# Queries loaded step by step, a sixth place for keys, a fourth for turned input, and spare products of the whole array in chunk 0 of an attention block

## The chip, the cores and the metric

The kernel runs on one core of one Trainium2 chip. A core has a matrix engine (TensorE, PE in the profile; its weight loads are PEld), VectorE (DVE), ScalarE (ACT), GpSimd (POOL), and SyncE (SP), which here issues every transfer. What is compared is device time in microseconds; lower is better.

## What is computed

One transformer layer on x of shape (2, 2048, 256): normalise, causal attention with 16 heads of 16 and 4 key heads, and beside it a linear map through the Fourier domain; both are added to x.

```python
xn = _layernorm(x)                          # x: (2, 2048, 256)
q = (xn @ wq).reshape(B, S, 16, 16); k = (xn @ wk).reshape(B, S, 4, 16); v = (xn @ wv).reshape(B, S, 4, 16)
q, k = _apply_rope(q, cos, sin), _apply_rope(k, cos, sin)
k, v = broadcast to 16 heads
scores = jnp.einsum('bshd,bthd->bhst', q, k) * scale    # causal mask, -inf above
out = jnp.einsum('bhst,bthd->bshd', softmax(scores), v).reshape(B, S, 256) @ wo
y = real(ifft(fft(xn) @ (w_re + i w_im))) + bias
x = x + out + y
```

## The kernel before

**Tiles.** The 4096 rows are cut into 8 chunks of 512 (`CHUNKS`), 4 for each of the two batches (`NJ`). In a chunk there are 4 steps, one for each key head, so 32 steps n, with n // 4 the chunk. Step n works on 4 heads, two in the upper half of the array's rows and two in the lower. Chunk 0 and chunk 4 see only themselves, chunk 3 and chunk 7 see four chunks of keys. A step has 4 x (j + 1) units (j the chunk's place in its batch), one for each tile of 128 keys.

**The work of a step.** First come the maxima ("a"): TensorE multiplies queries by keys into one of two pairs of banks in `psA`, and VectorE takes the maximum over each row (`reduce`, lines 1083 and 1085). Each such use has two halves (o = 1, 0). After the last one `shift` makes a value per row that SP carries back into the queries as two more rows (`load_shift`, 8 small transfers), so that the scores come out shifted. Then the scores ("b", line 1319) go into one of the three banks of `psS`, ScalarE takes their exponential (`exps`, line 956), GpSimd masks the diagonal, and the values product ("pv", line 1333) adds into `psO` over the units of a step: four matmuls side by side, each on 32 columns of the array (`VW`). `copy_sums` takes the finished sums to `oraw`, which has places for 8 steps.

**Around it.** For each chunk the input is normalised on GpSimd (`n`), turned ("t"), projected to keys and queries ("qk", line 1246, three of them) and values ("v"), and rotated on GpSimd in six steps (`rotate`). The rotated parts are stored to memory (`store`) and loaded again in another layout: `load_k` into one of `KS` = 5 places of `k_st`, `load_q` all four steps of a chunk at once into one of two halves of `q_st`. Both wait in SP's queue for the steps that use the old content (`pv_done`); a key load from chunk 5 on waits for all of batch 0. Behind the attention come "e", "e2", "e3": turn the sums, divide, project, and add to x.

**What sets the order.** `schedule()` simulates the engines with made-up durations and writes the order of TensorE, GpSimd and SP once and for all; ScalarE's and VectorE's follow from it. On the chip each engine runs its list in order, and a waiting instruction holds back all behind it. The opening (tables for the rotation, the Fourier weights, projections of chunk 0) is written by hand and stands ahead. VectorE reads the second batch's input for its moments right behind step 1's `shift` (`STATS_AT` = 1, lines 1034 and 1037), from `oraw`, which is still free.

## Time and profile before

| | us |
|---|---|
| median of 3 runs | 1062.55 (1062.13 to 1066.18) |
| the profiled execution | 1059.53 |
| its span, first to last instruction | 1057.5 |

A row of the profile's page gives an engine's busy time and its share of the span. A table of stretches gives, for windows counted from the span's start, how much each engine was busy in it and the clock that TensorE was granted, as a share of full speed. A row of the list in order of time gives start, duration, engine, line and tiles, how often, and in brackets how long the engine had been idle and who released it. A matmul of 32-bit numbers shows as two matmuls.

### The profile page before, as it was taken

The numbers are of one execution on the slowest core, as the hardware profiler recorded it, in microseconds if no ns is written. First come the engines' busy times: TensorE is split into PE (matmuls) and PEld (weight loads), VectorE is DVE, ScalarE is ACT, GpSimd is POOL, SyncE is SP. The second block draws the span as 40 slices with busy tenths as digits, with TensorE's granted clock in tenths as the row PEclk, the third lists the DMA queues.
The fourth block names the chain that finished last, engine by engine and source line by source line (L and its number), as shares of the span: only waits on it lengthen the run. The fifth ranks groups of instructions, "written<-read, shape, count | busy, mean of one in ns | idle before, by whom it ended". The sixth has DMA issues, their size and how long they took to land.

```text
span 1057.5 us, 17589 instructions
## 1 busy us (share of the span) xinstructions
PE 995.1 (94%) x6792; PEld 492.2 (47%) x6792; DVE 739.3 (70%) x893; ACT 651.8 (62%) x1303; POOL 321.7 (30%) x348
## 2 busy tenths in 40 slices
PE   8879799999999989999999899998999998999988
PEld 7635455444544434534444445444454443444434
DVE  6685867677678886778870367666768888778801
ACT  3324456646567745667777456663667774677785
POOL 6485851147380000183001258135010000110000
PEclk9866969999999979999999899988899997999999
DMA  5756070003610042100004314400700000000000
GB/s 159 139 145 74 31 111 11 13 20 83 99 36 17 1 59 32 42 22 30 2 4 54 47 42 87 65 3 30 111 22 1 2 1 1 12 11 2 1 1 20
DMA packets 35666, 43.46 MB, mean 41 GB/s; under 512 B 9344, under 2 KB 21248, under 8 KB 35584
## 3 DMA queue, kind: packets, MB, share of 16 engines
q1 hardware_dynamic: 35584, 42.35, 21.2%
q8 instruction: 53, 0.87, 0.3%
q14 instruction: 29, 0.24, 0.1%
HBM read 27.13 MB, written 14.68 MB: 40 GB/s over the span
## 4 chain that ended last, share of the span: by engine, by line
PE 80%; ACT 7%; DVE 7%; issue 3%; DMA 1%; POOL 1%; SPq 0%; ACTq 0%; POOLq 0%
PE psO L1333 27%; PE psA L1272 18%; PE psS L1319 17%; ACT prob_sb L956 5%; PE psS L1246 4%; DVE pmax L1085 3%; PE psS L1304 3%; PE psS L1306 2%; DVE pmax L1083 2%; PE psA L1277 2%; DMA q_st<-parts_scratch 1%; PE psS L1253 1%; PE psA L1287 1%; PE psO L1376 1%; ACT oraw_sb L965 1%
## 5 line engine op out<-in xcount | busy, mean ns | idle before, releaser
L956 ACT ACTIVATE prob_sb<-psS 128x512 f32<-128x512 f32 (+2 forms) x1108 | 561.7, 588 | 268.0 <-PE psS L1319 264.9
L1085 DVE TENSOR_REDUCE pmax<-psA 128x2 f32<-128x1024 f32 x384 | 458.6, 1220 | 117.7 <-PE psA L1272 116.6
L1319 PE MATMUL psS<-q_st,k_st 50*128 50x512 f32 (+3 forms) x1232 | 406.7, 440 | 8.4 <-ACT prob_sb L956 7.2
L1272 PE MATMUL psA<-k_st,q_st 48*128 48x512 f32 (+3 forms) x1280 | 371.4, 443 | 32.0 <-DVE pmax L1085 15.0
L1333 PE MATMUL psO<-prob_sb,v_sb 128*32 128x512 f32 (+3 forms) x2560 | 315.0, 566 | 12.5 <-ACT prob_sb L956 8.2
L1272 PEld LDWEIGHTS psA<-k_st,q_st 48*128 48x128 f32 x1280 | 180.7, 200 | 265.3 <-DVE pmax L1085 107.5
L1083 DVE TENSOR_REDUCE pmax<-psA 128x4 f32<-128x512 f32 (+2 forms) x192 | 198.9, 1043 | 97.1 <-PE psA L1277 95.6
L842 POOL TENSOR_SCALAR_AFFINE_SELECT prob_sb<-prob_sb 128x512 f32<-128x512 f32 x128 | 81.1, 636 | 562.9 <-ACT prob_sb L956 562.6
L1319 PEld LDWEIGHTS psS<-q_st,k_st 50*128 50x128 f32 x1232 | 200.2, 196 | 111.6 <-ACT prob_sb L956 101.1
L1333 PEld LDWEIGHTS psO<-prob_sb,v_sb 128*32 128x32 f32 x2560 | 51.6, 110 | 100.4 <-issue 43.1
L1277 PE MATMUL psA<-mask_r,mask_l 64*128 64x64 bf16 (+1 forms) x768 | 83.0, 217 | 0.0
L1246 PE MATMUL psS<-xnT,w_sb 128*128 128x512 f32 x96 | 50.9, 659 | 0.8 <-ACT xnT L911 0.8
L833 POOL TENSOR_TENSOR x_sb<-x_sb,back_sb 128x256 f32<-128x256 f32 x28 | 20.5, 731 | 84.7 <-ACT back_sb L941 84.7
L1277 PEld LDWEIGHTS psA<-mask_r,mask_l 64*128 64x128 bf16 x768 | 40.1, 103 | 11.9 <-issue 2.7
L919 ACT ACTIVATE qc<-psS 128x512 f32<-128x512 f32 x24 | 14.4, 599 | 49.4 <-PE psS L1246 46.6
L809 POOL TENSOR_TENSOR turn<-qc,cos_sb 128x512 f32<-128x512 f32 x21 | 26.7, 1272 | 48.8 <-ACT qc L919 47.4
L941 ACT ACTIVATE back_sb<-psS 128x256 f32<-128x256 f32 x28 | 10.8, 384 | 39.5 <-PE psS L1306 39.5
L1304 PE MATMUL psS<-m_sb,xnT 128*128 128x256 f32 x112 | 32.6, 415 | 0.0
L1113 DVE RECIPROCAL rl<-psA 128x32 f32<-128x32 f32 x14 | 5.0, 354 | 39.0 <-PE psA L1287 39.0
L789 POOL TENSOR_SCALAR xn<-x_sb,stat,rstd 128x256 f32<-128x256 f32 x24 | 29.0, 1224 | 4.9 <-PE psS L1238 3.9
L1189 DVE RECIPROCAL rl<-psS 128x16 f32<-128x16 f32 x4 | 1.0, 250 | 42.0 <-PE psS L1356 42.0
L1306 PE MATMUL psS<-wo_sb,back_sb 128*128 128x256 f32 x112 | 29.4, 386 | 0.0
(104 smaller groups left out, 582.9 us busy)
## 6 DMA issues: line engine op xcount, KB each, us to landing
q_st<-parts_scratch SPq DMA_DIRECT2D x42, 256.0 KB, 12.0
parts_scratch<-parts SPq DMA_DIRECT2D x64, 128.0 KB
k_st<-parts_scratch SPq DMA_DIRECT2D x48, 128.0 KB, 4.6
q_st<-spartT SPq DMA_DIRECT2D x256, 2.0 KB
x_sb<-in_L_attn_x SPq DMA_DIRECT2D x7, 512.0 KB, 4.2
out<-x_sb SPq DMA_DIRECT2D x14, 256.0 KB, 2.2
parts_scratch<-parts SPq DMA_DIRECT2D x32, 64.0 KB
oraw_sb<-in_L_attn_x SPq DMA_DIRECT2D x1, 2048.0 KB, 14.7
```

The costliest lines, as they stand in the source:

```text
L789: nc.gpsimd.tensor_scalar(xn[:, i, :], x_sb[:, xt(cc, i), :], stat[:, t, 0:1], rstd[:, t:t + 1], ALU.subtract, ALU.mult).then_inc(S["xn_re ...
L842: nc.gpsimd.affine_select(out=blk, in_=blk, compare_op=ALU.is_ge, fill=0.0, base=0, pattern=[[0, R], [1, P]], channel_multiplier=-1).then_ ...
L956: nc.scalar.activation(prob[:, g % DEEP, r0:r0 + hp, s0:CH], bank_at(bank)[:, 0:hp * w].rearrange("p (h s) -> p h s", h=hp), ACT.Exp).then ...
L1083: nc.vector.reduce_max(to, psA[:, two:two + 2, 0:per * w].rearrange("p o (h s) -> p o h s", h=per), AX.X).then_inc(S["a_free"], 1)
L1085: nc.vector.reduce_max(pmax[:, heads[0]:heads[0] + 3:2, i, q], psA[:, two:two + 2, :], AX.X).then_inc(S["a_free"], 1)
L1246: last = mm(bank, w_sb[:, c, block_cols(m)], xnT[:, cc % 3, c, :], start=(c == 0), stop=(c == KC - 1))
L1272: last = mm(bank[:, k * w:(k + 1) * w], q_st[lo:lo + ROWS, n % (2 * KV), heads[o * per + k] % 2, i * P:(i + 1) * P], k_st[lo:lo + ROWS, sl ...
L1277: last = mm(to, mask_l[lo:lo + HALF, h, :], mask_r[lo:lo + HALF, h:h + 1, :].broadcast_to([HALF, per, HALF]), start=False, stop=h == 1)
L1304: mm(bank[:, 0:D], xnT[:, cc % 3, c, t * P:(t + 1) * P], m_sb[:, c, :], start=(c == 0), stop=False)
L1306: last = mm(bank[:, 0:D], o_nT[:, i, c * P:(c + 1) * P], wo_sb[:, c, :], start=False, stop=(c == KC - 1))
L1319: last = mm(bank[:, h * w:(h + 1) * w], k_st[lo:lo + FULL, key_slot(n, tile), kv, tile % CT * P:(tile % CT + 1) * P], q_st[lo:lo + FULL, n ...
L1333: last = mm(psO[32 * r:32 * r + VW, s0:CH], v_sb[:, key_slot(n, tile) * CT + tile % CT, n % KV, :], prob[:, g % DEEP, r, s0:CH], start=(u ...
```

## The change

- `KS` goes from 5 to 6 places for keys, `xnT` from 3 to 4 for turned input (`XS`). The room comes from `oraw` (6 steps in place of 8, `OS`), `turn` (one row of 512 in place of two; the other product goes into `parts`), and from the value matrix, whose rows are 17 wide (`VW`) instead of 32. `psO` still holds four groups 32 apart (`GW`); VectorE clears it once at the start.
- Queries are loaded by step: 6 transfers of 64 KB for step n, waiting for step n - 8, each place with its own semaphore.
- Since a rotation's second product goes into `parts`, GpSimd waits for the store of two rotations earlier at the rotation's second step instead of its fifth. `copy_sums` waits for the turning of the sums of six steps earlier instead of eight. The second batch's input is read in two transfers, the second into the fourth place of `xnT`.
- `spare(at)` multiplies a 128x128 block of weights by 512 columns of input into the bank that the next real product will overwrite; nobody reads the result. Four stand ahead of the first maxima, and the planner puts one ("w") wherever, in its own reckoning, the next job of steps 0 to 3 is more than 0.6 us away and a bank is free. There are twelve of these: seven between the maxima from step 0's last to step 2's second, and five later up to step 2's scores.
- The planner takes all this into account, so the order changes everywhere.

The core of the diff:

```diff
-    KS = NJ + 1
+    KS = NJ + 2
+    XS = 4
+    OS = 6
+    TWO = OS * CH // D
...
+    SPARE_TO, SPARE_FROM, SPARE_TOOK = KV, 0.6, 0.87
+    OPEN_SPARES = 4
     LAG = 2
     DEEP = 3
-    VW = 32
+    VW = HD + 1
+    GW = 32
...
+                over = (chunk_begin(NJ) if cc >= KS else 0) if job[0] == "kload" else BEGIN[max(job[1] - 2 * KV + 1, 0)]
+                if len(pv_at) < over:
+                    continue
+                gate = max(gate, pv_at[over - 1] if over else 0.0)
                 if gate <= now:
-                    loads.remove(cc)
-                    issue_dma(gate, ("kload", cc))
-                    issue_dma(gate, ("qload", cc))
+                    loads.remove(job)
+                    issue_dma(gate, job)
...
-            return max(slot_ready(), q_ready.get(A_USES[next_a][1] // KV, big))
+            return max(slot_ready(), q_ready.get(A_USES[next_a][1], big))
...
+            if step < SPARE_TO and ready[choice if choice != "x" else "b"] > now + SPARE_FROM and bank_ready() <= now and a_part == 1:
+                pe.append(("w", len(ring)))
+                full("full", SPARE_TOOK, now)
+                continue
...
-        oraw_sb = sb("oraw_sb", [P, 2 * KV * CH], fp32)
-        oraw = oraw_sb[:, :].rearrange("p (n s) -> p n s", s=CH)
-        x_two = oraw_sb[:, :].rearrange("p (t n) -> p t n", n=D)
+        oraw = sb("oraw_sb", [P, OS, CH], fp32)
...
-        xnT = sb("xnT", [P, 3, KC, CH], fp32)
+        xnT = sb("xnT", [P, XS, KC, CH], fp32)
+        x_last = xnT[:, XS - 1, :, :].rearrange("p c s -> p (c s)").rearrange("p (t n) -> p t n", n=D)
...
-        turn = sb("turn", [P, 2, CH], fp32)
+        turn = sb("turn", [P, CH], fp32)
...
+            def load_q(n, t):
+                cc, g = n // KV, n % KV
                 m = 3 * cc + 1 + t
                 sp.wait_ge(stored[m % 2], 16 * (stores_before(m) + 4))
-                if cc >= 2:
-                    sp.wait_ge(S["pv_done"], chunk_begin(cc - 1))
+                if n >= 2 * KV:
+                    sp.wait_ge(S["pv_done"], BEGIN[n - 2 * KV + 1])
+                at = slice(t * P + 2 * g * HD, t * P + 2 * (g + 1) * HD)
                 for row, part in enumerate(PART_ROWS):
-                    slot = cc % 2 * KV
-                    sp.dma_start(q_st[t * HALF + row * HD:t * HALF + (row + 1) * HD, slot:slot + KV, :, :].rearrange("d g r s -> d (g r) s").bitcast(fp32),
-                                 scratch[cc, part, t * P:(t + 1) * P, :].rearrange("(h d) s -> d h s", d=HD)).then_inc(q_in[cc % 2], 16)
+                    sp.dma_start(q_st[t * HALF + row * HD:t * HALF + (row + 1) * HD, n % (2 * KV), :, :].bitcast(fp32),
+                                 scratch[cc, part, at, :].rearrange("(h d) s -> d h s", d=HD)).then_inc(q_in[n % (2 * KV)], 16)
...
-            sp.dma_start(x_two, x_v[:, BTILES:2 * BTILES, :]).then_inc(S["x_two_in"], 16)
+            sp.dma_start(x_two, x_v[:, BTILES:BTILES + TWO, :]).then_inc(S["x_two_in"], 16)
+            sp.dma_start(x_last, x_v[:, BTILES + TWO:2 * BTILES, :]).then_inc(S["x_two_in"], 16)
...
                 elif s == 1:
                     pool.wait_ge(S["turn_done"], base + 1)
-                    nc.gpsimd.tensor_tensor(turn[0:HALF, 1, :], qc[HALF:P, m % 2, :], sin_sb[HALF:P, span], ALU.mult).then_inc(S["turn_done"], 1)
+                    pool.wait_ge(stored[m % 2], 16 * stores_before(m))
+                    nc.gpsimd.tensor_tensor(other[0:HALF, :], qc[HALF:P, m % 2, :], sin_sb[HALF:P, span], ALU.mult).then_inc(S["turn_done"], 1)
...
+                if cc == XS - 1 and c == 0:
+                    act.wait_ge(S["bn_ready"], CHUNKS * CT)
+                if cc >= XS and c == 0:
+                    act.wait_ge(S["bank_full"], BANK["e3", cc - XS, 1, 1] + 1)
+                nc.scalar.activation(xnT[:, cc % XS, c, :], psS[:, BANK["t", cc, c] % RING, :], ACT.Copy).then_inc(S["bank_free"], 1)
...
-                if n >= 2 * KV:
-                    act.wait_ge(S["a_full"], back_job(2 * (n // KV - 2) + 1) + 1)
+                if n >= OS:
+                    act.wait_ge(S["a_full"], back_job(2 * ((n - OS) // KV) + 1) + 1)
...
+            nc.vector.memset(psO[:, :], 0.0).then_inc(S["psO_zeroed"], 1)
...
-                if m == 0 and n == 0 and o == 1:
-                    pe.wait_ge(S["q_first_in"], 96)
-                    pe.wait_ge(k_in[0], 96)
-                elif m == 0 and g == (1 if cc == 0 else 0) and o == 1:
-                    pe.wait_ge(q_in[cc % 2], 96 * (cc // 2 + 1))
-                    pe.wait_ge(k_in[cc % 2], 96 * (cc // 2 + 1))
+                if m == 0 and o == 1:
+                    if n in (0, 1):
+                        pe.wait_ge(q_in[n], 96)
+                    elif n >= KV:
+                        pe.wait_ge(q_in[n % (2 * KV)], 96 * q_loads(n))
+                    if g == 0:
+                        pe.wait_ge(k_in[cc], 96)
...
-                    last = mm(psO[32 * r:32 * r + VW, s0:CH], v_sb[:, key_slot(n, tile) * CT + tile % CT, n % KV, :], prob[:, g % DEEP, r, s0:CH],
-                              start=(u == 0), stop=(u == len(UNITS[n]) - 1), tile_position=(0, 32 * r))
+                    last = mm(psO[GW * r:GW * r + VW, s0:CH], v_sb[:, key_slot(n, tile) * CT + tile % CT, n % KV, :], prob[:, g % DEEP, r, s0:CH],
+                              start=(u == 0), stop=(u == len(UNITS[n]) - 1), tile_position=(0, GW * r))
...
+            def spare(at):
+                last = turn_before(at, LATE)
+                if last >= 0:
+                    pe.wait_ge(S["bank_free"], last + 1)
+                mm(bank_at(at), w_sb[:, 0, block_cols(0)], xnT[:, 0, 0, :], start=True, stop=True)
...
-                mm(psO[:, 0:P], ident[:, :], ident[:, :], start=True, stop=True)
+                mm(psA[:, 3, 0:P], ident[:, :], ident[:, :], start=True, stop=True)
...
+            for _ in range(OPEN_SPARES):
+                spare(len(OPENING))
...
+                elif job[0] == "w":
+                    spare(job[1])
```

What moves, at three places. TensorE, from the last maxima of step 0 to the first two of step 1. The rows `psA<-k_st,q_st` are maxima, `psA<-mask_r,mask_l` their mask. Before:

```order
L1272 MATMUL psA<-k_st,q_st 128x512 [waits a_free]
L1277 MATMUL psA<-mask_r,mask_l 128x64 x2
L1272 MATMUL psA<-k_st,q_st 128x128 [waits a_free,k_in_0,q_in_0]
L1272 MATMUL psA<-k_st,q_st 128x128
L1277 MATMUL psA<-mask_r,mask_l 128x2x64 x2
L1272 MATMUL psA<-k_st,q_st 128x128 [waits a_free]
```

Now, with line 1380 a spare product:

```order
L1300 MATMUL psA<-k_st,q_st 128x512 [waits a_free]
L1305 MATMUL psA<-mask_r,mask_l 128x64 x2
L1380 MATMUL psS<-xnT,w_sb 128x512 [waits bank_free]
L1300 MATMUL psA<-k_st,q_st 128x128 [waits a_free,q_in1]
L1300 MATMUL psA<-k_st,q_st 128x128
L1305 MATMUL psA<-mask_r,mask_l 128x2x64 x2
L1300 MATMUL psA<-k_st,q_st 128x128 [waits a_free]
L1300 MATMUL psA<-k_st,q_st 128x128
L1305 MATMUL psA<-mask_r,mask_l 128x2x64 x2
L1380 MATMUL psS<-xnT,w_sb 128x512 [waits bank_free]
```

A whole-array product now stands ahead of seven of the eight uses from step 1's first to step 2's second.

TensorE, step 0's scores (`psS<-q_st,k_st`) and first values (`psO<-prob_sb,v_sb`). Before:

```order
L1319 MATMUL psS<-q_st,k_st 128x384 [waits bank_free] x4
L1319 MATMUL psS<-q_st,k_st 128x256 [waits bank_free]
L1319 MATMUL psS<-q_st,k_st 128x256
...
L1272 MATMUL psA<-k_st,q_st 128x384 [waits a_free]
L1277 MATMUL psA<-mask_r,mask_l 128x64 x2
L1272 MATMUL psA<-k_st,q_st 128x384 [waits a_free]
L1277 MATMUL psA<-mask_r,mask_l 128x64 x2
L1333 MATMUL psO<-prob_sb,v_sb 32x512 [waits diag_masked]
L1333 MATMUL psO<-prob_sb,v_sb 32x512 x3
```

Now:

```order
L1347 MATMUL psS<-q_st,k_st 128x384 [waits bank_free] x4
L1364 MATMUL psO<-prob_sb,v_sb 17x512 [waits diag_masked,psO_zeroed]
L1364 MATMUL psO<-prob_sb,v_sb 17x512 x3
L1347 MATMUL psS<-q_st,k_st 128x256 [waits bank_free]
L1347 MATMUL psS<-q_st,k_st 128x256
...
L1364 MATMUL psO<-prob_sb,v_sb 17x384 [waits diag_masked]
L1364 MATMUL psO<-prob_sb,v_sb 17x384 x3
L1300 MATMUL psA<-k_st,q_st 128x384 [waits a_free]
L1305 MATMUL psA<-mask_r,mask_l 128x64 x2
```

Before, the first values product stood behind maxima that need a buffer back from VectorE (`a_free`), which by then reads the moments; now the first two value products stand ahead of the next maxima.

SP, around the last steps of chunk 3 (`q_st<-spartT` is `shift`, `k_st<-parts_scratch` a load of keys, `q_st<-parts_scratch` one of queries). Before, after the shifts of steps 15 to 19:

```order
L696 DMA q_st<-spartT 2x8x32 [waits spartT_ready]
L696 DMA q_st<-spartT 2x8x32 x7
L667 DMA k_st<-parts_scratch 16x4x512 [waits pv_done,ones_ready,stored_1]
L667 DMA k_st<-parts_scratch 16x4x512 x5
L677 DMA q_st<-parts_scratch 16x8x512 [waits pv_done,stored_0]
L677 DMA q_st<-parts_scratch 16x8x512 x2
L677 DMA q_st<-parts_scratch 16x8x512 [waits pv_done,stored_1]
L677 DMA q_st<-parts_scratch 16x8x512 x2
```

Now the same keys are loaded between queries of steps 18 and 19, ahead of step 12's shift:

```order
L698 DMA q_st<-parts_scratch 16x2x512 [waits pv_done,stored_1]
L698 DMA q_st<-parts_scratch 16x2x512 x2
L698 DMA q_st<-parts_scratch 16x2x512 [waits pv_done,stored_0]
L698 DMA q_st<-parts_scratch 16x2x512 x2
L687 DMA k_st<-parts_scratch 16x4x512 [waits ones_ready,stored_1]
L687 DMA k_st<-parts_scratch 16x4x512 x5
L717 DMA q_st<-spartT 2x8x32 [waits spartT_ready]
L717 DMA q_st<-spartT 2x8x32 x7
L698 DMA q_st<-parts_scratch 16x2x512 [waits pv_done,stored_1]
L698 DMA q_st<-parts_scratch 16x2x512 x2
L698 DMA q_st<-parts_scratch 16x2x512 [waits pv_done,stored_0]
L698 DMA q_st<-parts_scratch 16x2x512 x2
```

The key load no longer waits for `pv_done`; the queries are loaded for one step at a time. Counted in the order, 373 uses of maxima stood ahead of step 23's first scores and 389 do now (398 and 402 at step 24, 494 and 493 at step 28).

## Rows read from the trace of the kernel before

**Rows 1.** The page's first part for TensorE, and the list of cores.

```profile
PE 995.1 (94%) x6792; PEld 492.2 (47%) x6792; DVE 739.3 (70%) x893; ACT 651.8 (62%) x1303; POOL 321.7 (30%) x348
core 0: 1057.5 us, clock 0.932
```

**Rows 2.** Groups by line and shape: count, busy us, mean ns, idle before.

```profile
L1085 DVE TENSOR_REDUCE pmax<-psA 128x2 f32<-128x1024 f32 x384 | 458.6, 1220 | 117.7 <-PE psA L1272 116.6
L1272 PE MATMUL psA<-k_st,q_st 48*128 48x512 f32 x896 | 287.3, 476 | 16.4 <-DVE pmax L1085 11.7 <-DMA q_st<-parts_scratch 2.7 <-DVE pmax L1083 1.4
L1333 PE MATMUL psO<-prob_sb,v_sb 128*32 128x512 f32 x1792 | 249.9, 631 | 12.5 <-ACT prob_sb L956 8.2 <-ACT oraw_sb L965 2.6
```

**Rows 3.** Stretches: length, PE, PEld, DVE, ACT, POOL busy, clock, DMA.

```profile
61.00:96.00 35.00, 30.64 (x176) 17.22 (x176) 24.39 (x55) 12.96 (x27) 24.62 (x24) 0.50 0.65 101
71.00:74.40 3.40, 0.00 (x0) 0.00 (x0) 3.33 (x23) 0.62 (x2) 3.27 (x4) 0.50 0.14 34
101.60:124.80 23.20, 21.26 (x191) 11.44 (x190) 18.78 (x21) 16.03 (x32) 18.57 (x20) 1.00 0.07 21
124.80:129.30 4.50, 1.94 (x26) 1.02 (x18) 4.37 (x7) 0.00 (x0) 4.12 (x4) 0.94 0.22 75
129.30:152.30 23.00, 21.60 (x102) 10.93 (x102) 17.29 (x19) 10.77 (x21) 16.33 (x11) 0.50 0.84 122
```

**Rows 4.** TensorE in order of time, opening, and scores of steps 2 and 4.

```profile
38.68 1.88 PE L1246 MATMUL psS<-xnT,w_sb 128*128 128x512 f32 x4
...
44.40 0.70 PE L1272 MATMUL psA<-k_st,q_st 48*128 48x128 f32 x4 [3.84 <-issue]
...
46.05 3.78 PE L1246 MATMUL psS<-xnT,w_sb 128*128 128x512 f32 x4
...
101.73 0.73 PE L1319 MATMUL psS<-q_st,k_st 50*128 50x512 f32 x2
...
133.52 0.63 PE L1319 MATMUL psS<-q_st,k_st 50*128 50x512 f32 x2
```

**Rows 5.** SP in order of time: loads of chunk 1, shifts.

```profile
75.25 2.90 SPq L667 DMA_DIRECT2D k_st<-parts_scratch  x6
78.20 2.79 SPq L677 DMA_DIRECT2D q_st<-parts_scratch  x6
...
87.86 2.65 SPq L696 DMA_DIRECT2D q_st<-spartT  x4
...
126.58 5.22 SPq L696 DMA_DIRECT2D q_st<-spartT  x8
```

**Rows 6.** Transfers: count, KB each, median us from issue to landing.

```profile
q_st<-parts_scratch SPq DMA_DIRECT2D x42, 256.0 KB, 12.0
...
q_st<-parts_scratch SPq DMA_DIRECT2D x6, 64.0 KB, 2.5
```

**Rows 7.** SP and TensorE in order of time, between chunks 3 and 5.

```profile
570.60 2.68 SPq L667 DMA_DIRECT2D k_st<-parts_scratch  x6
...
591.19 0.50 PE L1272 MATMUL psA<-k_st,q_st 48*128 48x512 f32 x2 [2.69 <-DMA q_st<-parts_scratch]
```

**Rows 8.** Stretches later in the program, columns as in rows 3.

```profile
552.00:588.00 36.00, 32.79 (x214) 15.50 (x211) 1.11 (x3) 25.19 (x53) 5.89 (x9) 1.00 0.50 62
...
592.00:603.50 11.50, 11.50 (x65) 6.78 (x60) 5.60 (x5) 5.00 (x10) 1.91 (x3) 0.55 0.00 0
732.00:746.00 14.00, 9.68 (x52) 5.02 (x44) 12.85 (x15) 2.57 (x6) 4.22 (x4) 0.65 0.24 72
736.60:750.00 13.40, 11.88 (x54) 6.39 (x54) 10.47 (x10) 4.60 (x9) 0.00 (x0) 0.50 0.54 105
870.00:886.00 16.00, 12.13 (x68) 5.73 (x66) 14.25 (x17) 5.12 (x10) 0.00 (x0) 0.70 0.01 2
...
701.30:705.70 4.40, 3.92 (x24) 2.38 (x23) 3.66 (x4) 4.33 (x9) 3.35 (x4) 0.99 0.00 0
705.70:715.80 10.10, 10.10 (x46) 3.81 (x45) 4.37 (x4) 3.92 (x9) 4.86 (x5) 0.50 0.06 21
```

96 lines of the change are left out of this document (50 added, 46 removed).

## The prediction

> **What bounds the kernel now.** Read the page first, then the list of cores. TensorE has something to do in 94% of the span, and its mean granted clock is 0.932 [rows 1]. Since it has only the levels 1.2 and 2.4 GHz, about 2 x 0.068 x 1057.5 = 144 us pass at the lower one. So TensorE is the bound, and there are two things to win: its holes, and the time in which it does the same work at half speed. The next engine is VectorE, whose reduction over 1024 columns takes 1220 ns against some 0.5 us for the TensorE pair that feeds it [rows 2]: wherever TensorE has only such pairs left, it waits.
>
> The table of stretches shows where this happens first [rows 3]. From 61 to 96 us the clock is 0.50; TensorE shows 30.64 of 35 us busy, which would be about 15.3 at full clock, and VectorE needs 24.39. In the middle lies a hole of 3.40 us (71.0 to 74.4) in which VectorE reads the second half of the input. From 124.8 to 129.3 TensorE works 1.94 of 4.5 us, since VectorE is late, and then 23.00 us pass at 0.50 again, with 21.60 busy. The single instructions show the opening [rows 4]: TensorE waits 3.84 us for the first queries, and the projection behind it takes 3.78 us instead of 1.88. The scores of step 2 begin at 101.73, those of step 4 at 133.52.
>
> Later there are three more places. From 552 to 588 us VectorE has 1.11 us of work in 36 [rows 8]: chunk 5's maxima need its keys and queries, and those are fetched only once chunk 3 is through (570.60); TensorE waits 2.69 us for them [rows 7], and 592.0 to 603.5 runs at 0.55 [rows 8]. At the entries to chunks 6 and 7 VectorE is busy 12.85 of 14.00 and 14.25 of 16.00 us and TensorE only 9.68 and 12.13, with the clock at half behind the first [rows 8].
>
> **The opening.** Four spare products stand ahead of the first maxima. One is half of the row with four instructions, 1.88 / 2 = 0.94 us; four are 3.8 us in a hole of 3.84 [rows 4]. They cost 0 to 0.3 us. If they hold the clock, the 3.78 us become 1.9, and VectorE was waiting for this work: 1.9 us won.
>
> Behind it come seven spares between the maxima of steps 0 to 2. A pair takes about 0.7 us with its masks, a spare 0.94, together 1.6, against 0.7 to 1.2 us of VectorE: now and then TensorE is late. I count 0.9 us lost for the seven (bounds 0, where VectorE's buffer of two covers them, and 7 x 0.5 = 3.5). The net is 1.0 us by the end of step 1.
>
> **The rest of chunk 0.** In the new order the first value products no longer stand behind a product that waits for VectorE's moments, so 3.40 us of idle time [rows 3] are used. The clock is the larger part. Kept up, it would turn 30.64 us into 15.3, but VectorE's 24.39 us then bound the 35.00, so at most 10 us can be won; and five more spares (4.7 us) and eight pairs of step 4 (4 us) stand ahead of step 2's scores. These pairs are not extra, they leave later, the spares don't. Between the last spare of step 1 and the first values lie only scores and maxima, the same mix with which the clock was lost at 705.7 us, while TensorE was busy for 3.92 of 4.40 us [rows 8]. So I expect it to fall there too, for part of the stretch. I put step 2's scores at 101 to 107 us (101.73 before), but with eight pairs of maxima done ahead. From there to step 4's scores is some 22 us of work (23.20 before, [rows 3]), without the wait for VectorE: 123 to 129 us instead of 133.52. I take 127: **6.5 us won** (bounds 4 and 10).
>
> With step 4's maxima ready early the hole at 124.8 goes, and so may the 23.00 us at 0.50. At full clock the 21.60 us busy would be 10.8, but VectorE has 17.29 in them [rows 3]; at best 5.7 us are won, and I take **5** (bounds 0 and 5.7).
>
> **Queries step by step.** A load of 256 KB lands after 12.0 us, one of 64 KB in just the new shape after 2.5 [rows 6]. So a step's queries arrive some 10 us sooner. The price is issue time on SP: six issues take 2.79 us [rows 5], and a chunk now has 24, or 11.2 us: 8.4 more, and the maxima that SP carries into the queries (`shift`) are queued behind. In chunk 1 loads would end at 75.25 + 2.9 + 11.2 = 89.4 instead of 81; step 2's maxima, sent from 87.86 before, then go out from about 89.4. Step 4's went out at 126.58 and its scores began 6.9 us later [rows 4, 5], so step 2's scores are free at 96 to 97, still before TensorE comes to the scores (101 or later). Cost 0; if TensorE came there at 95 it would be 2. At chunk 2's entry SP has one query load, one store of four issues and one `shift` behind the last values of step 7, about 2.8 + 2 + 6.9 = 12 us; the TensorE order has about 18 us of other work there (five projections, four turnings and eleven pairs). Cost 0.
>
> The Trainium skill speaks against such a split: DMA: Bandwidth & Descriptors (Bandwidth) advises batching transfers to 1 MiB or more and calls small ones descriptor-dominated. The trace has both sizes, and 4 x 2.5 us is not more than 12.0 [rows 6]; by the rule the loads would land later and the next gain would be none.
>
> **One more place for keys.** With six places, chunk 5's keys don't wait for chunk 3 any more, and its first queries wait only for step 12. VectorE can then work in the 36 us in which it now has 1.11. What TensorE does is not less, so the gain is its idle 2.69 us and the 11.50 us at 0.55, of which 10 are at half clock and 5 are lost: 7.7, and I take **7.5** (bounds 2.7 and 9) [rows 7, 8].
>
> **Entries to chunks 6, 7 and 2.** By the new order 389 maxima are issued when step 23's scores begin, where there were 373, and step 24 needs 390. So the wait at 732 to 746 (14.00 - 9.68 = 4.3 us) should go, and with it the half clock (11.88 busy of 13.40, some 5 us) [rows 8]. I take **4**, for VectorE's 12.85 us were needed somewhere (bounds 0 and 9). Before step 28 the counts are 494 and 493 and only the way there is smoother: **1** (0 to 8). Chunk 2's inputs come earlier: 0.5 to 1, I take **1**.
>
> **Costed at nothing.** The value matrix is 17 wide instead of 32: its products stream the same 512 columns, 631 ns each [rows 2]. The clearing of psO and the second DMA of the input lie in VectorE's and SP's waits. GpSimd's wait for a store moves from the fifth step of a rotation to the second; behind it masks and additions are queued, for which the values wait, but the store is two rotations old. ScalarE's copy of the sums waits for the turning of the sums of six steps earlier, with exponentials behind it; in the TensorE order that turning stands ahead. If either wait bites, it is once in a chunk, some 1 us each: 0 to 8 us in all, and I take 0.
>
> The sum is 6.5 + 5 + 7.5 + 4 + 1 + 1 = 25 us. The profiled execution took 1059.53 us (span 1057.5), so it would take 1034.5; the median of the runs shown is 3.0 above it, and by the median the time is 1062.55 - 25 = 1037.5, or **1038 us**.
>
> **Rivals.** First, *the first chunk gives little*: the clock falls at step 0's scores and stays down to the first projection; the spares then cost 1.9 us apiece and take back what their holes gave. The gain is that of the later places and a little more, 14 us: 1048. For it speaks that TensorE was busy for 10.10 us on end at 0.50 without rising [rows 8].
>
> Second, *the holes only move*: VectorE and TensorE together have as much to do as before, and what is not waited for at one entry is waited for at the next: 1060. Against it speaks that VectorE is idle for 36 us on end.
>
> Third, on the other side, *the narrower values cost clock*. The clock was lost in a stretch that held only maxima and scores (50 rows of the array), and TensorE was busy in it [rows 8]. If the 128 x 32 value products are what holds it elsewhere, and if it is the columns at work in them that matter, 17 of 32 may not do. Each us at half clock costs up to half a us (3.78 against 1.88, [rows 4]), so from 2 x 25 = 50 us more at half clock the gain is gone; with 150 us more the time is 1038 + 75 = 1113. Nothing in this trace tells columns from array tiles.
>
> The Trainium skill gives another reading in TensorE: Matmul & The Clock Gate (Part 1): activity releases the throttle, whatever its kind. The trace does not agree, as TensorE was at 0.50 with 10.10 of 10.10 us busy; by that rule the third rival would be void and spares of any kind would do.
>
> **How the numbers follow.** Forecast (1025 to 1044) 0.42; more than that, where the entries to chunks 6 and 7 both clear, 0.12; little from the first chunk (1044 to 1056) 0.25; holes only move 0.08; narrower values or another new wait make it slower 0.13. For the range I leave out the slow case and the lowest few per cent: 1020 to 1062. The measurement of this kernel can tell about 0.5% (5.3 us) from no change: faster 0.79, same 0.08, slower 0.13.
>
> **What would show it.** Right: clock 1.0 at 46 to 50 us; step 2's scores at 101 to 107 and step 4's at 123 to 129; VectorE busy between chunk 3's end and chunk 5's start, no wait there for a query load; no wait for VectorE at chunk 6's entry. Wrong: a mean clock below 0.93, value products of 1.9 us in the later chunks (third rival); step 4's scores at 132 or later (first); `shift` loads late on SP behind query loads, with scores waiting for them.

## Result, and the profile after

| | median | runs | profiled span | mean clock |
|---|---|---|---|---|
| before | 1063.04 us | 1062.13 to 1066.18 | 1057.5 | 0.932 |
| after | 1022.62 us | 1017.43 to 1023.73 | 1020.8 | 0.958 |

The change makes the kernel faster by 3.9%: ratio 0.9614, 95% interval 0.9575 to 0.9652. The forecast was 1038 us, and the range of 1020 to 1062 holds the time. The sign was right; the gain was 40 us, not 25, and came from other places than forecast. Here and below a median is of all runs of a kernel, while a ratio leaves out those over 1.5% above its fastest, since the runs of one kernel can differ by 3% (1044.61 to 1074.18 us in e5).

The page after, for TensorE, with the granted clock in 40 slices, and the list of cores (to be set beside [rows 1]):

```profile
PE 982.8 (96%) x6824; PEld 475.0 (47%) x6824; DVE 732.6 (72%) x894; ACT 650.3 (64%) x1303; POOL 325.4 (32%) x350
...
PEclk9987789999989997999899999999999999999999
...
core 0: 1020.8 us, clock 0.958
```

TensorE is idle for 1020.8 - 982.8 = 38.0 us (62.4 before) and at half clock for 2 x 0.042 x 1020.8 = 86 us (144 before). Most of what is still lost stands in the first half: the last 20 slices all read 9.

Where the 36.7 us of span went shows in a table of stretches. Their bounds are the ends of steps, read from ScalarE's copy of the sums of steps 4, 11, 15, 23 and 27. The end of a step means this copy from here on. Columns: stretch, length, busy time of PE, PEld, DVE, ACT, POOL, clock, DMA share, GB/s. Before:

```profile
0.00:161.90 161.90, 141.11 (x886) 86.46 (x887) 114.47 (x222) 67.98 (x127) 100.30 (x102) 0.79 0.54 108
161.90:387.90 226.00, 215.93 (x1515) 103.66 (x1513) 175.84 (x184) 143.14 (x290) 79.59 (x82) 0.98 0.17 35
387.90:571.40 183.50, 178.11 (x1252) 80.51 (x1251) 127.21 (x141) 130.02 (x258) 41.07 (x43) 0.96 0.14 25
571.40:743.90 172.50, 160.62 (x1098) 83.45 (x1097) 104.73 (x118) 92.23 (x192) 74.58 (x81) 0.91 0.30 52
743.90:883.40 139.50, 133.04 (x932) 63.08 (x930) 113.67 (x119) 92.73 (x187) 13.09 (x20) 0.95 0.16 24
```

After, for the same steps:

```profile
0.00:161.50 161.50, 153.71 (x944) 90.37 (x945) 111.06 (x223) 70.13 (x133) 105.94 (x110) 0.87 0.42 101
161.50:396.40 234.90, 224.32 (x1524) 103.53 (x1523) 173.79 (x184) 143.69 (x290) 97.84 (x95) 0.96 0.23 55
396.40:579.60 183.20, 180.26 (x1318) 82.62 (x1317) 144.04 (x161) 129.65 (x258) 41.20 (x43) 0.96 0.07 22
579.60:717.40 137.80, 133.13 (x1018) 68.29 (x1017) 92.69 (x104) 89.69 (x189) 48.40 (x58) 0.99 0.14 35
717.40:847.10 129.70, 125.60 (x908) 56.77 (x906) 106.04 (x112) 91.60 (x185) 18.87 (x26) 0.99 0.14 32
```

- **Chunk 0 and step 4: 0.4 us.** TensorE is busier (153.71 of 161.5 against 141.11 of 161.9) and its clock better, 0.87 against 0.79, and yet the stretch is as long. A second profile of the changed kernel (e9 below) has 159.2 us here.
- **Steps 5 to 11: 8.9 us lost**, TensorE busy for 8.4 us more at a clock of 0.96 against 0.98.
- **Steps 12 to 15: 0.3 us.** But VectorE has 144.04 us of work here and not 127.21: maxima of chunk 5, done ahead.
- **Steps 16 to 23: 34.7 us.** Most of the gain is here. Of it 7 us are TensorE's idle time (11.9 against 4.7) and some 14 the half clock (2 x 0.09 x 172.5 = 31 us against 2 x 0.01 x 137.8 = 3, each us of them worth half a us, an estimate); the other 13 or 14 us are work that now stands earlier (1018 matmuls here against 1098, and 1318 against 1252 in steps 12 to 15).
- **Steps 24 to 27: 9.8 us**; steps 28 to 31: 0.4.

The first chunk in the order of time, TensorE after (compare [rows 4]); spares are L1380 (two matmuls each, so the four of the opening show as x8), maxima L1300, values L1364, scores L1347, projections L1273 and, for the values, L1280:

```profile
40.83 3.60 PE L1380 MATMUL psS<-xnT,w_sb 128*128 128x512 f32 x8
...
45.57 1.98 PE L1273 MATMUL psS<-xnT,w_sb 128*128 128x512 f32 x4
...
68.98 1.91 PE L1364 MATMUL psO<-prob_sb,v_sb 128*17 128x512 f32 x8 [1.38 <-POOL prob_sb L866]
...
115.98 2.39 PE L1280 MATMUL psS<-w_sb,xnT 128*128 128x64 f32 x10 [1.56 <-ACT prob_sb L982]
...
133.44 0.49 PE L1347 MATMUL psS<-q_st,k_st 50*128 50x512 f32 x1
```

And the stretches that answer to [rows 3] and [rows 8]; the second is the new one at half clock:

```profile
61.00:96.00 35.00, 32.79 (x204) 16.19 (x204) 24.27 (x60) 12.53 (x27) 25.33 (x23) 0.71 0.44 101
116.50:133.40 16.90, 16.58 (x98) 10.17 (x97) 9.39 (x14) 6.45 (x14) 9.43 (x10) 0.51 0.10 33
552.00:588.00 36.00, 35.51 (x308) 18.27 (x300) 28.55 (x36) 25.69 (x54) 3.83 (x7) 1.00 0.10 23
732.00:746.00 14.00, 13.77 (x110) 6.58 (x102) 10.38 (x11) 9.93 (x20) 1.41 (x3) 1.00 0.67 118
```

The opening went as forecast: four spares in 3.60 us, the projection at 45.57 in 1.98 us and not 3.78. But the clock falls just ahead of the first values (it is 0.73 from 68.0 to 68.5 us and 0.50 behind that), inside a hole of 1.38 us in which TensorE waits for GpSimd's mask. It falls again at 116.0 (0.52 from 116.0 to 116.5), at the end of a hole of 1.56 us in which TensorE waits for ScalarE to free a bank for the values' projection. In e9, the same kernel, the first fall comes just before 66 us, with TensorE busy for 0.94 of the 1.00 us ahead, and the second again at the end of the wait for ScalarE (1.58 us, until 113.69). Step 4's scores begin at 133.44 (133.52 before).

Later, two things have changed. SP after, at the keys of chunks 5, 6 and 7, and the keys of chunks 6 and 7 before (chunk 5's were issued at 570.60, [rows 7]):

```profile
360.07 2.72 SPq L687 DMA_DIRECT2D k_st<-parts_scratch  x6
...
585.31 2.70 SPq L687 DMA_DIRECT2D k_st<-parts_scratch  x6
...
735.96 2.88 SPq L687 DMA_DIRECT2D k_st<-parts_scratch  x6
```

```profile
651.68 2.71 SPq L667 DMA_DIRECT2D k_st<-parts_scratch  x6
...
743.34 2.82 SPq L667 DMA_DIRECT2D k_st<-parts_scratch  x6
```

Chunk 5's keys are fetched 210 us sooner, chunk 6's 66. And so VectorE isn't idle any more between 552 and 588 us. Its two long waits before, and its longest of that stretch after (start, length, what it does, idle time ahead and what ended it):

```profile
574.27 0.36 DVE L1113 RECIPROCAL rl<-psA 128x32 f32<-128x32 f32 x1 [23.22 <-PE psA L1287]
...
588.11 0.36 DVE L1113 RECIPROCAL rl<-psA 128x32 f32<-128x32 f32 x1 [12.69 <-PE psA L1287]
```

```profile
581.64 1.23 DVE L1111 TENSOR_REDUCE pmax<-psA 128x2 f32<-128x1024 f32 x1 [2.72 <-PE psA L1300]
```

A useful measure of this is VectorE's **lead**: how long before the end of step n - 1 the maxima of step n are complete (its `smax` row). For step 20 these rows are, before and after (step 19 ends at 629.14 and at 623.44):

```profile
618.05 0.18 DVE L1092 TENSOR_REDUCE smax<-pmax 128x16 f32<-128x32 f32 x1
```

```profile
576.36 0.19 DVE L1118 TENSOR_REDUCE smax<-pmax 128x16 f32<-128x32 f32 x1
```

At steps 20, 24 and 28, where chunks 5, 6 and 7 begin, the lead was 11.1, 9.6 and 9.4 us before; it is 47.1, 22.9 and 8.3 after. At step 8 it has become worse, from 2.1 to -5.3: there the last maxima now come after the end of step 7.

### The profile page after: what moved, and what is told of

Its sections match the earlier page's. It is cut to its first block, busy times and chain, and to the rows that moved or that the text cites. A ratio compares the mean times of both kernels' runs of the same rounds, so it can differ in the third digit from the quotient of the medians.

```text
span 1020.8 us, 17825 instructions
## 1 busy us (share of the span) xinstructions
PE 982.8 (96%) x6824; PEld 475.0 (47%) x6824; DVE 732.6 (72%) x894; ACT 650.3 (64%) x1303; POOL 325.4 (32%) x350
## 4 chain that ended last, share of the span: by engine, by line
PE 82%; ACT 7%; DVE 3%; issue 2%; POOL 1%; DMA 1%; SPq 1%; POOLq 0%; ACTq 0%; DVEq 0%
PE psO L1364 28%; PE psA L1300 19%; PE psS L1347 17%; ACT prob_sb L982 5%; PE psS L1273 3%; PE psS L1332 3%; PE psS L1334 2%; DVE pmax L1111 2%; PE psA L1305 2%; PE psA L1315 1%; PE psS L1280 1%; DVE pmax L1109 1%; ACT oraw_sb L991 1%; PE psA L1347 1%; PE psS L1265 1%
## 5 line engine op out<-in xcount | busy, mean ns | idle before, releaser
L1111 DVE TENSOR_REDUCE pmax<-psA 128x2 f32<-128x1024 f32 x384 | 459.6, 1220 | 134.1 <-PE psA L1300 132.7
L1347 PE MATMUL psS<-q_st,k_st 50*128 50x512 f32 (+3 forms) x1232 | 403.5, 431 | 5.0 <-ACT prob_sb L982 3.5
L1300 PE MATMUL psA<-k_st,q_st 48*128 48x512 f32 (+3 forms) x1280 | 362.3, 427 | 7.8 <-DVE pmax L1111 5.0
L1364 PE MATMUL psO<-prob_sb,v_sb 128*17 128x512 f32 (+3 forms) x2560 | 310.4, 558 | 15.2 <-ACT prob_sb L982 7.5
L1300 PEld LDWEIGHTS psA<-k_st,q_st 48*128 48x128 f32 x1280 | 177.6, 192 | 252.4 <-DVE pmax L1111 96.4
L1347 PEld LDWEIGHTS psS<-q_st,k_st 50*128 50x128 f32 x1232 | 196.8, 192 | 96.3 <-ACT prob_sb L982 84.0
L1364 PEld LDWEIGHTS psO<-prob_sb,v_sb 128*17 128x17 f32 x2560 | 43.2, 96 | 106.1 <-issue 44.8
L1305 PE MATMUL psA<-mask_r,mask_l 64*128 64x64 bf16 (+1 forms) x768 | 79.2, 210 | 0.0
L1273 PE MATMUL psS<-xnT,w_sb 128*128 128x512 f32 x96 | 46.8, 614 | 0.8 <-ACT xnT L937 0.8
L837 POOL TENSOR_TENSOR parts<-qc,sin_sb 64x512 f32<-64x512 f32 x21 | 26.7, 1271 | 6.1 <-DMA parts_scratch<-parts 3.7
## 6 DMA issues: line engine op xcount, KB each, us to landing
oraw_sb<-in_L_attn_x SPq DMA_DIRECT2D x1, 1536.0 KB, 11.9
```

The costliest lines, as they stand in the source:

```text
L1111: nc.vector.reduce_max(pmax[:, heads[0]:heads[0] + 3:2, i, q], psA[:, two:two + 2, :], AX.X).then_inc(S["a_free"], 1)
L1273: last = mm(bank, w_sb[:, c, block_cols(m)], xnT[:, cc % XS, c, :], start=(c == 0), stop=(c == KC - 1))
L1300: last = mm(bank[:, k * w:(k + 1) * w], q_st[lo:lo + ROWS, n % (2 * KV), heads[o * per + k] % 2, i * P:(i + 1) * P], k_st[lo:lo + ROWS, sl ...
L1305: last = mm(to, mask_l[lo:lo + HALF, h, :], mask_r[lo:lo + HALF, h:h + 1, :].broadcast_to([HALF, per, HALF]), start=False, stop=h == 1)
L1347: last = mm(bank[:, h * w:(h + 1) * w], k_st[lo:lo + FULL, key_slot(n, tile), kv, tile % CT * P:(tile % CT + 1) * P], q_st[lo:lo + FULL, n ...
L1364: last = mm(psO[GW * r:GW * r + VW, s0:CH], v_sb[:, key_slot(n, tile) * CT + tile % CT, n % KV, :], prob[:, g % DEEP, r, s0:CH], start=(u ...
```

## Experiments

All ratios are to the kernel before, timed beside them on the same chip; 1% is 10.6 us. The table below has them in one place. The planner lays out a new order for each kernel that is told of another limit, so "a part undone" is that part with the order that goes with it; only the runs in which the text says so keep the order. What an order alone can be worth is 7 us, plus or minus 7 (e10 and e11).

| label | key places | input places | queries released | spares | median us | ratio (95%) |
|---|---|---|---|---|---|---|
| changed kernel, first time | 6 | 4 | by step | 4 + 12 | 1022.62 | 0.9614 (0.9575 to 0.9652) |
| e9, changed kernel again | 6 | 4 | by step | 4 + 12 | 1018.39 | 0.9597 (0.9563 to 0.9631) |
| e1 | 6 | 4 | by step | none | 1010.85 | 0.9552 (0.9474 to 0.9631) |
| e2 | **5** | 4 | by step | 4 + 12 | 1030.70 | 0.9746 (0.9674 to 0.9818) |
| e3 | 6 | **3** | by step | 4 + 12 | 1067.25 | 1.0074 (1.0033 to 1.0114) |
| e4 | 6 | 4 | **by chunk** | 4 + 12 | 1045.89 | 0.9859 (0.9795 to 0.9923) |
| e5 | 5 | 3 | by chunk | none | 1051.22 | 0.9886 (0.9852 to 0.9919) |
| e6 | 5 | **4** | by chunk | none | 1035.29 | 0.9769 (0.9720 to 0.9818) |
| e7 | 5 | 3 | **by step** | none | 1066.71 | 1.0053 (1.0028 to 1.0079) |
| e8, values 32 wide | 5 | 4 | by step | 4 + 12 | 1049.33 | none given |
| e10 | 6 | 4 | by step | none | 1012.27 | 0.9563 (0.9526 to 0.9601) |
| e11, order of the changed kernel | 6 | 4 | by step | **left out** | 1024.09 | 0.9630 (0.9579 to 0.9682) |
| e12 | 6 | 4 | by step | 4 + 0 | 1008.52 | 0.9553 (0.9508 to 0.9598) |

### One part undone: spares, key place, input place, release of the queries

**e1.**

```diff
-    SPARE_TO, SPARE_FROM, SPARE_TOOK = KV, 0.6, 0.87
-    OPEN_SPARES = 4
+    SPARE_TO, SPARE_FROM, SPARE_TOOK = 0, 0.6, 0.87
+    OPEN_SPARES = 0
```

> The changed kernel without its spare matmuls, neither the four in the opening nor those that the planner puts in holes of the first chunk; the other parts stay. The comparison of the two traces has the start of the copy of step 4's sums at 161.94 us before and 161.48 after, so the first chunk gave nothing by there. Theory A (the spares are worth about nothing, since the clock falls between them all the same): 1020 to 1026 us, with the first projection of chunk 1's third block back near 3.8 us (it took 3.78 before and 1.98 after). Rival B (the spares hold the clock through steps 0 and 1, and the shorter opening, 82.11 against 89.69 us at the end of step 0, is theirs, and what the planner did with it later too): 1027 to 1035 us.

Measured: 1010.85 us, which neither theory had: without spares the kernel was not as fast but, by the ratios, some 0.6% faster, with intervals that overlap. The first projection of chunk 1's third block took 2.94 us, on the way to the 3.8 expected. This is taken up again in e9 to e12.

**e2.**

```diff
-    KS = NJ + 2
+    KS = NJ + 1
```

> The changed kernel with five places for keys and values in place of six; queries, input places, width and spares as changed. The planner is told that the keys of chunk 5 wait for the end of step 15, and lays out its order by that. Theory A (the sixth key place frees the entry to the second batch, which is where the time went: from the end of step 15 to the end of step 19 the kernel before took 57.7 us and the changed one 43.8): 14 us of the gain go, 1033 to 1040 us, with the wait of TensorE near 591 us on the keys' transfer back, at a half clock behind it. Rival B (the fourth input place does the work, by letting the stages run further ahead): within 5 us of the changed kernel, 1018 to 1028 us.

Measured: 1030.70 us, ratio 0.9746 against 0.9597 to 0.9614 for the changed kernel: the sixth key place is worth 14 to 16 us in this company. Chunk 5's keys are issued at 558.65, at the end of step 15, and VectorE waits for them again:

```profile
558.65 2.65 SPq L687 DMA_DIRECT2D k_st<-parts_scratch  x6
```

```profile
562.32 0.36 DVE L1139 RECIPROCAL rl<-psA 128x32 f32<-128x32 f32 x1 [21.34 <-PE psA L1315]
```

Theory A's size was right (14 us expected; its 1033 to 1040 us was missed by 2 on the low side), its place only half: the wait of TensorE for a transfer is 1.0 us and not 2.69, and the lead at step 24 falls from 22.9 to 11.3 us too.

**e3.** The fourth place stays in memory, for the last tiles of the statistics' input.

```diff
+    XM = 3
-   ... xnT[:, cc % XS, ...]
+   ... xnT[:, cc % XM, ...]
-                if cc >= XS:
-                    at = max(at, e3_at.get((cc - XS, 1, 1), big))
+                if cc >= XM:
+                    at = max(at, e3_at.get((cc - XM, 1, 1), big))
```

> The changed kernel with the normed input's places used in turns of three, as before; the fourth holds only the last tiles of the second batch for the statistics. Six key places, queries by the step, narrow values and spares stay. Theory A (the fourth place carries the entries to chunks 5, 6 and 7: steps 20 to 27 took 107.4 + 7.4 us more in the kernel before, of 254.3 against 223.7): about 25 to 30 us of the gain go, 1045 to 1053 us, with the half clock back at the entries to chunks 6 and 7. Rival B (key place and queries by the step do it, and the fourth place only shifts work between stages that are full anyway): 1018 to 1030 us.

Measured: 1067.25 us. All of the gain is gone, and more: 49 us, where theory A had 25 to 30. (Steps 20 to 27 took 254.3 us before and 223.7 after, 30.6 less; the "107.4 + 7.4" of the expectation is a slip.) The rows name the mechanism: chunk 6's keys are issued at 706.52 (585.31 after the change, 651.68 before it), VectorE has nothing to do for 63.63 us, and when the work comes TensorE, ahead with everything else, waits for it at half clock.

```profile
706.52 2.80 SPq L686 DMA_DIRECT2D k_st<-parts_scratch  x6
```

```profile
718.12 1.23 DVE L1108 TENSOR_REDUCE pmax<-psA 128x2 f32<-128x1024 f32 x1 [63.63 <-PE psA L1297]
```

```profile
740.00:750.00 10.00, 6.33 (x26) 2.70 (x26) 10.00 (x10) 0.00 (x0) 0.01 (x1) 0.66 0.96 149
750.00:760.00 10.00, 6.76 (x30) 3.10 (x28) 9.56 (x13) 0.00 (x0) 0.00 (x0) 0.50 0.76 115
```

The lead at step 24 is -32.8 us. Chunk 5's maxima were early (lead 50.9 at step 20): with key place and queries released, VectorE ran ahead into chunk 5 and then stood still for chunk 6. This is the "holes only move" of the forecast's second rival, with its price.

**e4.** The loads keep their size and their number; only what they wait for is as before.

```diff
-                    sp.wait_ge(S["pv_done"], BEGIN[n - 2 * KV + 1])
+                    sp.wait_ge(S["pv_done"], chunk_begin(cc - 1))
```

> The changed kernel whose loads of queries still go one step at a time (four pairs of transfers a chunk), but all four of a chunk wait for the same thing as before the change, the end of the chunk two before it, and the planner is told so. Theory A (release by the step matters where the queries' places come free late, at each entry to a chunk, since the next chunk's loads otherwise all start at its last moment): 10 to 20 us of the gain go, 1033 to 1043 us. Rival B (what was late at the entries was keys and input, the queries of the next chunk having their places a whole chunk ahead): within 4 us of the changed kernel, 1018 to 1027 us.

Measured: 1045.89 us, 26 to 28 us more by the ratios; theory A, and more than it said. Here the sixth key place is of no use: chunk 5's keys are long there (issued at 343.51), but its queries go out when step 15 is through, in one burst of 24, and VectorE waits 23.12 us as in the kernel before.

```profile
572.41 12.29 SPq L698 DMA_DIRECT2D q_st<-parts_scratch  x24
```

```profile
576.09 0.36 DVE L1139 RECIPROCAL rl<-psA 128x32 f32<-128x32 f32 x1 [23.12 <-PE psA L1315]
```

The leads at steps 20, 24 and 28 are 12.7, 9.7 and 9.4 us, those of the kernel before.

### One part alone

**e5.** The small edits only, among them the queries' loads of 64 KB in place of 256; e6 and e7 each add one part to it.

```diff
-    KS = NJ + 2
+    KS = NJ + 1
+    XM = 3
-    SPARE_TO, ... = KV, ...    OPEN_SPARES = 4
+    SPARE_TO, ... = 0, ...     OPEN_SPARES = 0
-                    sp.wait_ge(S["pv_done"], BEGIN[n - 2 * KV + 1])
+                    sp.wait_ge(S["pv_done"], chunk_begin(cc - 1))
```

> Only the small edits of the change: values 17 columns wide with the cleared bank, the rotation's sum kept in one half of parts, six places for the copied sums, four pairs of query transfers a chunk but all released by the chunk's end as before. Five key places, three input places, no spares. Theory A (width and the rest cost nothing by themselves, as the forecast took it; the gain is in the three large parts): within 0.5% of the kernel before, ratio 0.995 to 1.005. Rival B (the narrow values do something of their own: they give the array less to do in a step and the clock falls more often, or they free it sooner): outside that, ratio over 1.01 or under 0.99.

Measured: ratio 0.9886: 12 us faster, so rival B, on its good side. What was costed at nothing is worth over 1%. Where the 12 us lie can't be read: the profiled run took 1074.18 us, the longest of the eleven.

**e6.** e5 with `xnT[:, cc % XS, ...]` again, four places. The stores of the output also count on one semaphore for each chunk.

> The kernel of the run on the small edits, with the fourth input place added and nothing else (its stores of the output count on one semaphore for each chunk, which moves no work). Theory A (the fourth input place is what lets the parts of chunks 5, 6 and 7 be made a chunk earlier; taking it away cost 48 us against the changed kernel, all of its gain): it gives at least half of the gain alone, 1030 to 1045 us, ratio 0.97 to 0.985. Rival B (the parts work only together: parts made early still wait for the fifth key place and for queries released by the chunk): less than a quarter of the gain, 1052 to 1062 us, ratio over 0.99.

Measured: 1035.29 us, ratio 0.9769. Theory A's figure, but beside e5 it is 16 us by the medians, 12 by the ratios, and not 25: the rest are the small edits. VectorE still waits for chunk 5's keys (issued at 557.84), since there are five places:

```profile
561.50 0.36 DVE L1142 RECIPROCAL rl<-psA 128x32 f32<-128x32 f32 x1 [21.32 <-PE psA L1318]
```

**e7.** e5 with the wait on `BEGIN[n - 2 * KV + 1]` again.

> The kernel of the run on the small edits, with the queries released by the step and nothing else: five key places, three input places, no spares. Theory A (queries released by the step are worth something only if a chunk's parts exist before its queries' places come free, which needs the fourth input place; the changed kernel with three input places took 1067 us although it had the release by the step and six key places): 1055 to 1070 us, ratio 0.995 to 1.01. Rival B (the release by the step is worth its 26 us, what taking it away cost, by itself): 1030 to 1042 us, ratio under 0.985.

Measured: 1066.71 us, ratio 1.0053, and beside e5 18 us slower by the ratios. Rival B is out; theory A holds, and it is worse than nothing: chunk 6's keys go out at 696.63 (651.68 before), VectorE is idle for 33 us ahead of 712.51. Why they go out later than before stays open.

```profile
712.51 2.36 DVE L1108 TENSOR_REDUCE pmax<-psA 128x2 f32<-128x1024 f32 x2 [33.32 <-PE psA L1297]
```

What follows from e2 to e7: **the three parts are links of one chain** (input to keys and queries, to maxima, to scores), and what one is worth depends on the others. Releasing queries by the step costs 18 us with three input places and five key places (e5 to e7) and wins 26 to 28 with all else in place (e4 to the changed kernel). The sixth key place wins 14 to 16 us with queries by the step (e2 to the changed kernel); it was not run alone, but without the fourth input place nothing of it is seen: e3, with six places, has 1.0074, and e7, with five, 1.0053 (e3 has the spares too). The input place wins 12 us by itself (e5 to e6). Each figure includes the new order that came with it.

**e8.** e2 with the values 32 columns wide. No instruction changes its place.

```diff
-    VW = HD + 1
+    VW = 32
```

> The changed kernel with five key places, and the values 32 columns wide again, as in the kernel before: a value matmul then loads and writes 32 columns for each head in place of 17, in the same order of instructions on every engine. With six key places the memory doesn't hold them. To be set beside the run with five key places alone (ratio 0.9746). Theory A (width is worth nothing; the array takes a matmul's time by the columns of prob that stream, 512, whatever the width of what it holds): ratio 0.970 to 0.980. Rival B (narrow values cost clock, the third case of the forecast, or save weight loads that stand before matmuls): the two ratios differ by over 0.01.

Measured: 1049.33 us, but no ratio can be given, since the runs fall apart: three of the four had a mean clock of 0.938 to 0.946 and took 1048.9 to 1055.2 us, the fourth 0.965 and 1033.0. Three of the runs of e2 (0.962 to 0.967) took 1029.5 to 1031.5. At equal clock, by that one run and on another chip, the width would be worth 1.5 to 3.5 us. Whether narrow values also keep the clock up more often, which was rival B and would be worth far more, four runs don't tell. What a row can tell is the duration at full clock, 430 to 510 us, where both traces grant 1.00 (line, shape, count, busy us, mean ns, idle). Values of e2, then of e8:

```profile
L1364 PE MATMUL psO<-prob_sb,v_sb 128*17 128x512 f32 x200 | 26.3, 598 | 1.6 <-ACT prob_sb L982 0.8 <-ACT oraw_sb L991 0.5
```

```profile
L1364 PE MATMUL psO<-prob_sb,v_sb 128*32 128x512 f32 x200 | 26.6, 604 | 1.5 <-ACT prob_sb L982 0.8 <-ACT oraw_sb L991 0.5
```

200 of them take 26.3 us against 26.6; for all 2560 value products that is some 4 us (estimate, 2560 / 200 x 0.3). The weight loads take 95 ns against 107, beside other work. So of e5's 12 us some 4 may be the shorter products. The rest was not separated: what the width does to the clock, the loads of 64 KB, which land after 2.5 us where those of 256 KB took 12.0 [rows 6], the rotation with one buffer less, and the order that goes with six places for the copied sums.

### The spares

Four kernels on one chip, six runs each. e11 keeps every row of the changed kernel's order and drops its sixteen spares; e12 is e10 with the opening's four.

```diff
 # e11
-    OPEN_SPARES = 4
+    OPEN_SPARES = 0
 ...
                 elif job[0] == "w":
-                    spare(job[1])
+                    continue
```

> The changed kernel once more, as the measure of the three runs beside it on the same chip: ratio 0.957 to 0.965 by every theory, since the first comparison gave 0.9614.

> The changed kernel planned and run without any spare, as in the first run of this study (ratio 0.9552). Theory A (the twelve spares of the planner stand in front of work that could run, and the order that the planner lays around them is a worse one for the steps 8 to 11, where the changed kernel ended 10 us behind this one): 6 to 12 us under the changed kernel beside it, ratio 0.950 to 0.956. Rival B (the first run was a chance, the spares being worth nothing either way): within 3 us of the changed kernel.

> The changed kernel with its order of all other work kept exactly, and only its sixteen spare matmuls left out, four of the opening and twelve of the planner. Theory A1 (it is the order that costs, not the matmuls): as slow as the changed kernel, within 3 us. Theory A2 (it is the matmuls, twelve by some 0.9 us on TensorE in steps 0 and 1): as fast as the kernel planned without spares, 6 to 12 us under the changed kernel. Rival B (the spares do hold the clock where they stand, at full clock to 68.5 us, and pay for themselves there): 2 to 8 us over the changed kernel.

> The kernel planned without spares, with the four spares of the opening alone put back; every other row is the same. Theory A (they hold the clock over the opening's gap, so that the first projection of chunk 1's third block takes 1.98 us and not 3.78, but the clock falls all the same at the first values, near 68 us, so that at most 2 us of it stay): within 2 us of the kernel without spares, to either side. Rival B (they delay the first maxima by their own 3.6 us and VectorE with them): 2 to 5 us over it.

Measured: 1018.39 (e9), 1012.27 (e10), 1024.09 (e11), 1008.52 us (e12). By the ratios, with intervals put together from theirs: e11 is 7 us slower than e10 (plus or minus 7), so **the order laid around the spares seems to cost**, whether they run or not; six runs each put this at the edge of what can be told, and the rows below speak for it. e11 is 3.5 slower than e9 (6.5): in their places the spares rather pay, which is e11's rival B, though the interval takes in zero. e9 is 3.6 slower than e10 (5.3), less than theory A's 6 to 12 and hardly more than rival B's 3; in the first comparison, on two chips, the changed kernel was 6.6 slower than e1. e12 is 1 faster than e10 (6), so the opening's four are worth nothing that can be told, as expected (the projection behind them takes 1.98 us in e12 and 3.78 in e10).

What the spares do in step 0 and what that is worth (columns as above; the stretches end with step 0). e9, e10, e11:

```profile
0.00:79.80 79.80, 75.74 (x445) 50.25 (x446) 56.88 (x157) 30.83 (x54) 48.14 (x57) 0.91 0.64 157
```

```profile
0.00:80.80 80.80, 70.03 (x419) 48.78 (x420) 56.94 (x157) 30.49 (x54) 48.19 (x57) 0.83 0.61 151
```

```profile
0.00:82.20 82.20, 70.60 (x423) 50.12 (x424) 58.54 (x157) 30.97 (x54) 48.00 (x57) 0.82 0.60 150
```

TensorE's idle time falls from 11 us to 4 and its clock rises by 0.08 or 0.09, and the step ends 1.0 to 2.4 us sooner (one profile each, and that of e11 is of a run of 1031.19 us). That is all: VectorE has 57 to 58.5 us of work here in each, and TensorE was waiting for it and for GpSimd, at either clock.

Where the order costs is steps 8 and 9 (e9, then e10):

```profile
232.70:283.30 50.60, 47.87 (x331) 25.76 (x331) 40.20 (x47) 27.20 (x57) 20.71 (x22) 1.00 0.24 60
283.30:321.90 38.60, 37.17 (x239) 15.39 (x238) 26.84 (x28) 24.54 (x50) 13.49 (x13) 0.91 0.11 32
```

```profile
230.50:276.70 46.20, 44.37 (x319) 24.83 (x319) 35.89 (x40) 26.23 (x54) 20.72 (x22) 1.00 0.24 64
276.70:312.00 35.30, 34.37 (x237) 15.24 (x236) 26.92 (x28) 25.69 (x53) 16.32 (x15) 1.00 0.13 38
```

7.7 us in two steps, of the 10.7 by which e9 is behind at the end of step 23 (711.95 against 701.23); in step 9 the lower clock, 0.91 against 1.00, is part of it. In step 8 VectorE has 47 operations against 40: the order with spares has left more maxima for it, and its lead at step 8 is -5.3 us against 2.1. Counted in the order, 100 of the 102 maxima that step 8 needs stand ahead of step 7's last values, where the kernel before and e10 have all 102. e11 has the same 47 operations (its step 8 takes 50.5 us). Steps 5 to 11 take 234.9 us in both profiles of the changed kernel and 225.2 to 227.8 in those of e1, e10 and e12 (226.0 before). Spares don't bring this with them everywhere: e2, with sixteen spares and five key places, has all 102 in place and takes 227.4 us there.

**The best version** is therefore the change without the planner's spares: e10 and e12, with ratios of 0.9563 and 0.9553 and medians of 1012.3 and 1008.5 us, are the fastest here. That leaving the planner's spares out beats the changed kernel too, by some 4 to 7 us, was seen three times with one sign (e1, e10, e12), but no interval shuts out zero.

## Why the prediction was right, and where it was wrong

That the time fell within the range is in part luck. Of 36.7 us of span, the terms measured 0.4 (first chunk, 11.5 forecast), -8.6 (steps 5 to 15, +1), 13.9 (key place, 7.5), 20.8 (entry to chunk 6, 4), 9.8 (chunk 7, 1) and 0.4 behind it: some 21 us too much at the front was more than made up by some 32 too little later. The steps one by one:

- **First chunk, 6.5 + 5 us: measured 0.4 by the end of step 4.** Here the first rival was right. The clock did fall between the last spare of step 1 and the first values, as the text said (among busy scores at 66 us in e9, inside the hole of 1.38 us in the first profile), and step 2's scores began at 104, within the 101 to 107. The step that failed is the next: "some 22 us of work" from there to step 4's scores took 29.4, since the clock fell again at 116.0, and from 116.5 on 16.9 us went by at 0.51. The forecast had taken the wait for VectorE as the only thing that drops the clock there; now it fell at the end of a wait of 1.56 us for ScalarE, and in e9 too. The 22 us became 29.4 in both. The spares' balance by the end of step 1 was put at 1.0 us; with equal order it is 1.2 (102.88 in e9, 104.05 in e11, one profile each). But the order without spares does no worse: step 4 ends at 157.9 us in e10, 158.7 in e1 and 160.2 in e12, against 159.2 and 161.5 with them. The hole of 3.84 us in the opening stands in [rows 4] as "issue"; that it was a wait for the queries was read from the order, and behind the spares the row does name their transfer (0.46 us in e12).
- **Steps 5 to 15: 1 us for chunk 2's inputs, measured 8.6 lost.** The inputs don't come earlier: SP issues chunk 2's keys at 153.17 and not 134.46. And chunk 2's entry lost its lead. No row of the kernel before shows this; the counts of maxima in the new order do (100 of 102 ahead of step 7's last values), and the forecast counted them for steps 24 and 28, but not for step 8. That is the real omission: the spares were charged their own time and not the order laid around them. Without them, in e10, steps 5 to 15 take 407.1 us, 2.4 less than before.
- **One more place for keys, 7.5 us: measured 13.9 by the end of step 19** (from 8.2 us behind to 5.7 ahead), and 14 to 16 by e2. Place and mechanism held: 35.51 us of 36 are busy, VectorE has 28.55 in them and not 1.11, and TensorE waits for no transfer longer than 0.2 us. The size was cut to TensorE's idle and half-clock time of one stretch [rows 7, 8]; the maxima done in VectorE's free time were counted as worth nothing, "what TensorE does is not less". But it was idle for 3.2 of the 36 us and now for 0.5, and each of these maxima (1220 ns, [rows 2]) is one that nobody waits for in steps 16 to 23.
- **Entry to chunk 6, 4 us: measured 20.8** (5.7 to 26.5). Direction right, size far off. The count of 389 maxima where 390 are needed was right, and from 670 to 750 us TensorE shows no wait for VectorE at all. The upper bound of 9 was taken from the two stretches at 732 to 750, as if steps 20 to 22 weren't touched; they gave 3.2 us, and step 23 alone 17.7. The half clock at 705.7 to 715.8 [rows 8] lies in that step and is gone too; the forecast had it only as an example of a lost clock, not as something to win.
- **Entry to chunk 7, 1 us: measured 9.8.** This lies outside even the bound of 8, and in steps 24 to 27, not at the entry itself, where the lead of 9.4 us is 8.3 now: VectorE comes to these steps with more in hand (leads of 17.1 to 24.6 us at steps 24 to 27, and 9.6 to 17.0 before).
- **Queries by the step, cost 0 on SP: held.** 24 issues take 12.14 us, and the shifts of steps 2 and 3 go out at 87.27 (87.86 before). The worth of the release was put inside the key place's term, and by e4 it is 26 us or more, by e7 less than nothing alone.

```profile
75.09 12.14 SPq L698 DMA_DIRECT2D q_st<-parts_scratch  x24
87.27 13.47 SPq L717 DMA_DIRECT2D q_st<-spartT  x16
```

```profile
q_st<-parts_scratch SPq DMA_DIRECT2D x174, 64.0 KB, 2.5
```

  The last row lists the loads after: 174 of 64 KB, 2.5 us each. The Trainium skill advises to batch transfers to 1 MiB or more (DMA: Bandwidth & Descriptors, Bandwidth), and calls descriptor-dominated only those under 64 KB, which these are not. No run has the split alone. With it and the other small edits the kernel was 12 us faster (e5), and with the size kept, the moment at which a load may start was worth 26 us or more (e4).
- **Costed at nothing:** small edits at 0, measured 12 us won (e5). So the 0 to 8 us feared for the waits that were moved on GpSimd and ScalarE were at least outweighed; they were not measured by themselves.
- **Third rival, narrow values cost clock:** it did not slow the kernel. The mean clock rose to 0.958, and the last 20 slices are at 0.9 or above. Whether the width does anything to the clock stays open (e8).

The first rival (first chunk gives little) came true together with the case that had 0.12 (both entries clear, 1020 to 1025). They had been listed as exclusive; they are separate questions, and the cases should have been crossed. Case 0.12 was also sized too small: steps 16 to 27 gave 44.5 us.

## What to carry to other kernels

Where a slower engine (here VectorE) feeds a faster one, read its lead at each boundary before its idle time: how long before it is needed its last piece is ready. Follow one late piece back through every buffer that it passes and widen them together; beside e5, one link alone lost 18 us (queries), another won 12 (input), and all three won some 34 (e10). And when spare work is added by a planner, take it out again with the order kept: what it costs may be the order around it.

## What was not expected of the hardware

- **The same order at another clock.** e9 and e11 have the same instructions in step 6, and TensorE is idle for 0.6 and 0.5 us in it. One runs it at 1.00, the other (a run of 1031.19 us) at 0.73, and it takes 24.3 and 31.5 us:

```profile
182.90:207.20 24.30, 23.70 (x171) 11.05 (x170) 15.53 (x18) 16.53 (x34) 14.61 (x15) 1.00 0.11 34
```

```profile
187.20:218.70 31.50, 31.02 (x171) 13.54 (x170) 15.71 (x18) 16.51 (x34) 14.59 (x15) 0.73 0.08 26
```

  The Trainium skill says that activity releases the throttle (TensorE: Matmul & The Clock Gate, Part 1). Here TensorE was busy throughout from 190 to 205 us of e11 and stayed at 0.50; it was back at 1.00 only by 210. Nor is it the stretch before: step 5 took 23.7 and 23.8 us in the two, at 1.00 in both, with TensorE busy for 23.53 and 23.64, and ahead of the fall both wait the same 0.5 us for ScalarE. What decides was not found. So a clock lost in one profile needn't be lost in the next, and no single one prices a stretch.
- **Scatter by the clock.** Six runs of e12 on one chip took 1006.71 to 1019.60 us at mean clocks between 0.946 and 0.961. Of two versions that are 4 us apart, six runs of each don't settle which is faster.
- **Narrow values** take 598 ns against 604 for the same 512 columns at full clock, and their weight load 95 ns against 107 (e2 and e8, 430 to 510 us).
